# A split-precision cross-attention kernel: seventeen products per context piece in place of eighteen, a stacked last tile, and a new order at the seam

## The reference

```python
def mha(q, k, v):            # 8 heads, softmax(q k^T / sqrt(80)) v
    ...
enc, ca = ctx[:, :718], ctx[:, 718:]
hs = mha(x @ Wq, enc @ Wk, enc @ Wv)
ca_q1 = einsum('btc,th->bch', ca, Wq_ca)[:, linspace(0, 383, 100)]
ca_hs1 = mha(ca_q1, x, x)
ca_hs2 = mha(ca_hs1 @ Wq, ca @ Wk_ca, ca @ Wv_ca)
out = (hs + ca_hs2) @ Wout + b_out + x
```

## Time and profile before

| | us |
|---|---|
| median of 3 runs | 1008.68 |
| lowest and highest | 1005.97, 1013.66 |
| profiled execution, its own time | 1004.1 |
| its span, first to last instruction | 1002.4 |
| TensorE busy | 983.8 (98%) |
| VectorE, ScalarE, GpSimd busy | 645.5, 490.0, 343.5 |
| mean granted TensorE clock | 0.992 |

### The profile page before, as it was taken

The page is one execution under the profiler, slowest core; times in us unless marked ns, Lnnn a source line. Parts: engine busy times, 40 slices in busy tenths (PEclk is TensorE's granted clock), DMA queues, the critical chain, the costliest instruction groups (busy, mean ns, idle before and its releaser), DMA issues.

```text
span 1002.4 us, 20729 instructions
## 1 busy us (share of the span) xinstructions
PE 983.8 (98%) x6740; PEld 964.2 (96%) x6740; DVE 645.5 (64%) x1129; ACT 490.0 (49%) x895; POOL 343.5 (34%) x286
## 2 busy tenths in 40 slices
PE   9999799999999999999999999999999999999998
PEld 9998699999999999999999999999999999998997
DVE  6444556676667766767676767676766666667444
ACT  7433445555454546464646463646454545546110
POOL 5212254424251616151524243343343343416000
PEclk9899999999999999999999999999999999999999
DMA  7989967797978797979797978888787878795354
GB/s 266 258 285 279 259 131 203 168 196 172 195 172 191 174 182 178 185 184 179 185 186 176 186 191 169 202 174 201 161 208 157 206 163 202 168 216 156 97 181 146
DMA packets 154169, 190.12 MB, mean 190 GB/s; under 512 B 80928, under 2 KB 108192, under 8 KB 154144
## 3 DMA queue, kind: packets, MB, share of 16 engines
q1 hardware_dynamic: 147456, 177.44, 75.9%
q10 hardware_dynamic: 6688, 12.35, 3.7%
HBM read 81.56 MB, written 19.95 MB: 101 GB/s over the span
## 4 chain that ended last, share of the span: by engine, by line
PE 85%; SPq 5%; DMA 4%; DVE 3%; ACT 2%; issue 1%; ACTq 0%
PE psS L750 22%; PE psB L785 20%; PE psB L790 10%; PE psS L725 8%; PE psT L766 6%; PE psS L894 6%; PE psT L812 4%; PE psT L818 2%; SPq L382 2%; DMA kstack<-kT 1%; PE psB L867 1%; PE psB L844 1%; SPq L379 1%; PE psT L819 1%; PE psS L950 1%
## 5 line engine op out<-in xcount | busy, mean ns | idle before, releaser
L750 PE MATMUL psS<-encT_keep,Wk_keep 128*128 128x360 f32 x1440 | 255.3, 330 | 2.8 <-ACT probs L1133 2.8
L750 PEld LDWEIGHTS psS<-encT_keep,Wk_keep 128*128 128x128 f32 x1440 | 238.7, 189 | 3.9 <-issue 3.3
L785 PE MATMUL psB<-PT_h,encN_h 120*128 120x400 f32 x576 | 202.3, 351 | 0.0
L785 PE MATMUL psB<-PT_l,encN_h 120*128 120x400 f32 x576 | 198.8, 345 | 0.0
L1133 ACT ACTIVATE probs<-psS,negmax 100x718 f32<-100x718 f32 x128 | 110.2, 861 | 131.8 <-DVE negmax L1524 131.6
L612 POOL TENSOR_TENSOR encT_keep<-encT_raw,encT_keep 128x718 fp32r<-128x718 f32 x45 | 79.7, 1770 | 184.6 <-ACT encT_keep L1162 182.2
L1548 DVE TENSOR_TENSOR kT<-psS,kT 128x718 fp32r<-128x718 f32 x80 | 72.4, 905 | 105.7 <-ACT kT L1157 105.7
L620 POOL TENSOR_TENSOR encN_l<-enc_raw,encN_h 120x768 fp32r<-120x768 f32 x48 | 92.4, 1926 | 93.5 <-ACT encN_h L1169 92.1
L603 POOL TENSOR_TENSOR Mbd<-Mbd,fmask 128x320 fp32r<-128x320 f32 x48 | 47.0, 978 | 221.4 <-DMA Mbd<-m_split 218.8
L1157 ACT ACTIVATE kT<-psS 128x718 fp32r<-128x718 f32 x80 | 61.7, 771 | 123.4 <-PE psS L750 109.9
L790 PE MATMUL psB<-PT_h,encN_l 120*128 120x400 f32 x576 | 120.4, 344 | 0.7 <-POOL encN_l L620 0.7
(11 more groups left out here) (245 smaller groups left out, 1635.8 us busy)
## 6 DMA issues: line engine op xcount, KB each, us to landing
kstack<-kT SPq DMA_DIRECT2D x64, 448.8 KB
kstack<-kT SPq DMA_DIRECT2D x192, 112.2 KB
enc_raw<-in_encN_dram SPq DMA_DIRECT2D x48, 360.0 KB, 5.5
encT_raw<-in_encT_dram SPq DMA_DIRECT2D x45, 359.0 KB, 6.0
kstack<-kT SPq DMA_DIRECT2D x32, 359.0 KB
kstack<-kT SPq DMA_DIRECT2D x32, 269.2 KB
kstack<-kT SPq DMA_DIRECT2D x32, 179.5 KB, 3.6
kstack<-kT SPq DMA_DIRECT2D x64, 89.8 KB, 3.9
```

Source lines behind the costliest of these rows:

```text
L750: mm = pe.matmul(keys_in(f, first)[:, half, 0:HALF], w[:, c, f * 128:(f + 1) * 128], e[:, c, k0:k0 + HALF], start=(j == 0), stop=(j == 3 * ...
L785: pe.matmul(psB[:, 1, 0:RH], eN[0][:, k, cc], PT[p][:, k, rows], start=(k == 0 and p == 0), stop=False)
```

## The change

Key tiles become 128 keys: five full ones (FULLK = 5) and a tail of TAIL = 78. The tail's three products (high-high, high-low, low-high) are folded into two by stacking: rows 78 to 116 of the tail tile, which were unused, hold half of the third product. So `context` has 5 x 2 + 5 + 2 = 17 products. For that

- `norm` writes the first 39 tail keys a second time beside the tail (a new small VectorE instruction for each head), so that the transposes bring them to rows 78 to 116;
- `enc_high` takes key tiles 4 and 5 first (`third`), `enc_twice` (ScalarE) writes the tail's high part into the low buffer too, `enc_low` (GpSimd) has four instructions and makes the tail's low part in place first;
- two DMAs on SP (`tail_enc`) put the tail's low part into the unused rows of both context buffers, one on SP (`tail_pt0`) and one on ScalarE's queue (`tail_pt1`) put 39 rows of the high probabilities into `PT[1]`, for either half of the heads; `context` waits for them just ahead of its last two products (u = 0 for the context, u = 0 and 3 for the probabilities).

Besides: SP issues `load_q(i + 1)` ahead of `lift(i + 1, 0)`; `scores(i, 1)` with its maximum and exponential moves behind `context(i - 1, 2)`; in batch 0 the loads of the next contexts take their ordinary places between the lifts, and `expo(0, 5)` goes ahead of `q_high(3, 5)`; the forty small products are dealt out 7, 7, 7, 7, 6, 6; the context of batch 0 is loaded into another buffer, as soon as Wk has left it, and split ahead of heads 6 and 7.

```diff
-KP = (KEYS + KT - 1) // KT
+KP = 128
-HALF = KPAD // 2
+HALF = 360
+FULLK = KEYS // KP
+TAIL = KEYS - FULLK * KP
+TH = TAIL // 2
+TSTK = TAIL + TH
...
+        LOWS = PARTS + 1
+        tail_low = enc_raw[0:KP, FULLK * C:KT * C].bitcast(F32R)
-        enc0_raw = P_keep[:, 0:CT * KEYS].rearrange("p (c k) -> p c k", c=CT)
+        enc0_raw = rawT
...
+        def third(c):
+            return slice(4, 6) if c == 0 else slice(2 * (c - 1), 2 * c)
...
                 def load_enc(b, c, first=False):
-                    free("encN", PARTS * (b - 1) + c + 1, first)
-                    ks = slice(c * KQ, (c + 1) * KQ)
+                    free("encN", LOWS * (b - 1) + c + 2, first)
+                    if c == 0:
+                        free("entail", 32 * b, first)
+                    ks = third(c)
...
+                def tail_pt0(b):
+                    wait_apart(sp, s["ptlo"], HEADS * b + 4, s["passed_sp"])
+                    sp.dma_start(raw(PT[1][TAIL:TSTK, FULLK, 0:RH]), raw(PT[0][TH:TAIL, FULLK, 0:RH]))\
+                      .then_inc(s["pttail"], 16)
+                def tail_enc(b):
+                    wait_apart(sp, s["encN"], LOWS * b + 1, s["passed_sp"])
+                    for p in range(2):
+                        sp.dma_start(raw(eN[p][TAIL:TSTK, FULLK, :]), raw(tail_low[p * TH:(p + 1) * TH, :]))\
+                          .then_inc(s["entail"], 16)
...
                 load_ga(0, first=True)
+                sp.wait_ge(s["wlo"], 5)
+                sp.dma_start(enc0_raw, encT[0].rearrange("(c p) k -> p c k", p=128)).then_inc(s["encin"], 16)
                 sp.wait_ge(s["hlo"], 6)
                 load_heads(6, 2)
                 sp.wait_ge(s["v2st"], 32)
                 load_q(0, first=True)
-                sp.wait_ge(s["hlo"], HEADS)
-                sp.dma_start(enc0_raw, encT[0].rearrange("(c p) k -> p c k", p=128)).then_inc(s["encin"], 16)
...
                 lift(0, 2, heads=(3,), first=True)
-                sp.wait_ge(s["wlo"], 5)
-                for c in range(CT):
-                    load_encT(1, c, first=True)
-                for c in range(PARTS):
-                    wait_apart(sp, s["xTlo2"], 3 * FT, s["passed_sp"])
-                    load_enc(0, c, first=True)
-                load_ga(1)
+                sp.wait_ge(s["enc0lo"], CT)
...
                     if first:
                         sp.wait_ge(s["encT"], PARTS)
                         sp.dma_start(wv_raw, tiled(Wv)).then_inc(s["wvin"], 16)
                         load_q(i + 1)
-                    else:
+                    tail_pt0(i)
+                    tail_enc(i)
+                    if not first:
                         wait_apart(sp, s["hsp"], 2 * i, s["passed_sp"])
                         load_v2(i)
                         if not last:
                             store_hs(i - 1, 1)
                     if not last:
-                        lift(i + 1, 0)
                         if not first:
                             load_q(i + 1)
+                        lift(i + 1, 0)
                         lift(i + 1, 1)
...
                 def enc_low(b):
-                    for c in range(PARTS):
...
+                    pool.wait_ge(s["encNhi"], LOWS * b + 2)
+                    nc.gpsimd.tensor_tensor(tail_low, rawN[:, FULLK, :], eN[0][:, FULLK, :],
+                                            ALU.subtract).then_inc(s["encN"], 1)
+                    pool.wait_ge(s["encN"], LOWS * b + 1)
+                    nc.gpsimd.tensor_tensor(eN[1][:, FULLK - 1, :], rawN[:, FULLK - 1, :], eN[0][:, FULLK - 1, :],
+                                            ALU.subtract).then_inc(s["encN"], 1)
+                    for c in range(1, PARTS):
...
-                for c in range(3):
+                for c in range(2):
                     wo_low(c)
                 enc_low(B - 1)
...
-                    for k in range(KT):
+                    for k in range(FULLK):
                         for p in range(2):
                             pe.matmul(psB[:, 1, 0:RH], eN[0][:, k, cc], PT[p][:, k, rows],
                                       start=(k == 0 and p == 0), stop=False)
-                    for k in range(KT):
-                        if u == 0 and k % KQ == 0:
-                            pe.wait_ge(s["encN"], PARTS * i + k // KQ + 1)
-                        mm = pe.matmul(psB[:, 1, 0:RH], eN[1][:, k, cc], PT[0][:, k, rows],
-                                       start=False, stop=(k == KT - 1))
-                    mm.then_inc(s["u"], 1)
+                    for n, k in enumerate((4, 0, 1, 2, 3)):
+                        if u == 0 and n in (0, 1, 3):
+                            pe.wait_ge(s["encN"], LOWS * i + (n + 1) // 2 + 2)
+                        pe.matmul(psB[:, 1, 0:RH], eN[1][:, k, cc], PT[0][:, k, rows], start=False, stop=False)
+                    if u == 0:
+                        pe.wait_ge(s["entail"], 32 * i + 32)
+                    if c == 0:
+                        pe.wait_ge(s["pttail"], 32 * i + 16 * half + 16)
+                    pe.matmul(psB[:, 1, 0:RH], eN[0][0:TSTK, FULLK, cc], PT[0][0:TSTK, FULLK, rows],
+                              start=False, stop=False)
+                    pe.matmul(psB[:, 1, 0:RH], eN[1][0:TSTK, FULLK, cc], PT[1][0:TSTK, FULLK, rows],
+                              start=False, stop=True).then_inc(s["u"], 1)
...
                         context(i - 1, 2)
+                        scores(i, 1)
                     keys(i, 3)
...
                         b2_scores(i + 1, 1)
-                        scores(i + 1, 1)
...
+                def enc_twice(b):
+                    nc.scalar.activation(eN[1][0:TAIL, FULLK, :], rawN[0:TAIL, FULLK, :], ACT.Copy)\
+                      .then_inc(s["encNhi"], 1)
+                def tail_pt1(b):
+                    act.wait_ge(s["ptlo"], HEADS * b + HEADS)
+                    act.dma_start(raw(PT[1][TAIL:TSTK, FULLK, RH:R]), raw(PT[0][TH:TAIL, FULLK, RH:R]))\
+                      .then_inc(s["pttail"], 16)
...
                     if first:
                         store_q2(4, FT)
                         store_g2()
+                    else:
+                        u_high(i - 1, 2)
+                        expo(i, 1)
+                    k_high(i, 3)
...
                     xm_copy(i)
+                    expo(i, 5)
                     if first:
                         q_high(3, 5)
                         enc_high(i, 0, first)
+                        enc_twice(i)
                         store_q3(5)
-                    expo(i, 5)
...
+                    nc.vector.tensor_scalar(P[h % PRING][0:S, KEYS:KEYS + TH],
+                                            P[h % PRING][0:S, FULLK * KP:FULLK * KP + TH], inv[:, h:h + 1],
+                                            None, ALU.mult).then_inc(s["inv"], 1)
...
                         u_low(i - 1, 2)
+                        rowmax(i, 1)
+                    k_low(i, 3)
                     norm(i, 1)
-                    k_low(i, 3)
```

More of the change, by code:

```diff
@@ L497, in batch @@
                         load_enc(i, 1)
-                    elif not first:
-                        load_encT(i + 1, 1)
+                    else:
+                        load_encT(i + 1, 1, first)
                     if not first:
@@ L513, in batch @@
                         load_wo(1)
-                    elif not first:
-                        load_enc(i, 1)
-                        load_enc(i, 2)
-                    if not last and not first:
+                    else:
+                        load_enc(i, 1, first)
+                        load_enc(i, 2, first)
                         load_ga(i + 1)
-                    if not last:
                         load_x(i + 1)
@@ L1081, in _ @@
                 turn_ca_keys()
-                for j, heads in enumerate(((0,), (1, 2), (3,), (4,), (5,), (6, 7))):
+                parts = (0, 7, 14, 21, 28, 34, 40)
+                for j in range(NP):
                     query(1, j)
-                    for h in heads:
-                        m_head(h)
+                    m_parts(parts[j], parts[j + 1])
                 query(2, 0)
@@ L1296, in batch @@
                 def batch(i, first=False, last=False):
-                    if not first:
-                        u_high(i - 1, 2)
-                    k_high(i, 3)
                     if first:
@@ L1449, in _ @@
                 q_high(1, 2)
+                for c in range(CT):
+                    enc0_high(c)
                 head_high(6)
@@ L1453, in _ @@
                 q_high(1, 4)
-                for c in range(CT):
-                    enc0_high(c)
                 q_high(1, FT)
@@ L1807, in _ @@
                 q_low(1, 2)
+                for c in range(CT):
+                    enc0_low(c)
                 head_low(6)
@@ L1811, in _ @@
                 q_low(1, 4)
-                for c in range(CT):
-                    enc0_low(c)
                 q_low(1, FT)
```

65 lines of the change are left out of this document (38 added, 27 removed).

## The result

| | before | after |
|---|---|---|
| median (4 runs each) | 1009.95 | 1051.91 |
| lowest and highest | 1005.97, 1013.66 | 1038.95, 1059.53 |
| ratio, 95% interval | | 1.038 [1.0335, 1.0425] |
| span of the profiled execution | 1002.4 | 1037.2 |
| mean granted TensorE clock | 0.992 | 0.976 |

A forecast was written before the change was run, and what follows sets the result against it. TensorE was taken as the bound inside the loop. Fewer products (-17.6), the net of (a) to (e) (-5.8) and the last batch (+0.5) gave -22.9 from 1004.1, 981.2; plus 4.6 for the median, 985 us, range 974 to 1000.

The forecast's parts named there:

- The tail's DMAs in the loop: SP's three tail loads per batch, wanted by the stacked products: slack 1.4 to 3 us, later SP issues covered by 5; nothing.
- q ahead of lift 0: SP's loop order: last lift piece just in time for keys 2; nothing, bounds 0.1 us gain to 1 us loss per batch.
- Rival 1: Every batch: late lifts or a late exponential cost 0.5 to 1 us in 15 batches, total 993 to 1000; chance 0.13.
- third rival: Context 0, products 16 and 17: tail DMAs late in every batch, slow clock after, 57 us in all, total 1042; chance 0.07.
- Scores 1 behind a context piece: Loop, scores 1 moved: exponential 1 still ready for scores 2 with 0.4 to 1 us to spare; zero gain or loss.
- One product less: Each context piece on TensorE: one product fewer, 16 batches x 6 pieces x 0.184 = 17.6 us saved, bounds 17 to 18.
- (c): Before keys 3 of batch 0: exponential 5 moved ahead removes the 2.81 wait and slow products after it, -4.6 us.
- (e): Batch 0, context 0: new wait of 4.2 us for the tail's DMAs behind q, plus slow stretch, +5.8 us (2.5 to 7).
- (d): Forty small products before batch 0, dealt in even lots: part of the clock loss from 34 to 46 us regained, -1.5 (0 to -3.4).
- (a): Batch 0's context loaded and split elsewhere: ends the wait at 81.79 and the slow stretch after it, -3.8 us (0 to -4.2).
- (b): Batch 0, lift 2 (head 4): bulk loads no longer ahead of it, -1.7 us of the wait at 105.47 (0 to -3).
- Last batch: Context 0 of the last batch wants GpSimd's split parts 0.5 us earlier: costs 0.5 us (0 to 2).

## Why the prediction was wrong, step by step

**The tail's DMAs in the loop: the step that failed.** The landing was right (the wait stands in batch 0 alone). The sentence behind it was wrong: "Queued behind this wait on SP are V2, the output store, q and lift 0, whose first issue starts only at 549.93: covered by 5 us." It set 544.8 against 549.93 and left out V2 and the store between them, 2.5 and 0.4 us and their gaps. The cover was the 1.5 us in which SP stood still, against three issues of 0.8 with gaps, 2.6 us in all, where 0.48 each had been read from a load of another shape. Lift 0 began 1.1 to 1.3 us later against TensorE. That the queue ahead of the lift is the cause is shown by the kernel that keeps q ahead and only moves V2 and the store (with GpSimd's spread of V2): -41.5 us. In the kernel with the products alone the same lateness makes q late in place of the lift, and the loop gains nothing (730.0 for 729.1).

**q ahead of lift 0.** "Just in time" was nearly right for SP as it stood before: the copy of keys 2 was 1.0 us later, and the total some 5 us longer. But the margin was 0.1 us and the step before had already spent it. The two hang together: with q put back, or V2 and the store out of the way, 40 us come back (1051.9 to 1011.5 or 1010.4). I summed two terms of zero, each worked out with the other's slack unspent.

**Rival 1** named this chain and priced it at 0.5 to 1 us per batch; it was 53.86 - 50.85 = 3.0 against the forecast period; 0.7 of this is the 51.57 that its best batch reached, where the moved scores 1 have their part. The price lacked the stretch at the low clock: 2.2 us of waiting had 2.7 of slow products behind it. The third rival had that factor, for another wait; that its 1042 came near the measured time is luck, for the stacked products of the loop never waited.

**Scores 1 behind a context piece.** Zero was wrong: 0.5 to 0.6 us per batch alone (52.57 for 52.08 in the mean, and 52.55 for 51.92 in the steady batches). The text asked only what scores 1 would wait for, not what had been running beside it in its old place. With turn 7 in the gap the wait goes.

**One product less, transposes, small VectorE instruction.** Right: 0.17 to 0.18 per piece and 51.0 as the lowest period, against 50.85. By the Trainium skill ("TensorE: Matmul & The Clock Gate", LDWEIGHTS), which has the load's time as columns / 1.2 ns, each load would be an estimated 7 ns longer. The traces show nothing of it in the pace: six transposes still take 0.46 from their start to that of the next instruction. The 39-column instruction takes 0.25 alone but 1.08 beside GpSimd, so "surely under 0.56" was wrong there.

**The seam.** (c) right, no wait at keys 3 of batch 0. (e) right in place and near in the wait, 4.86 for 4.2, but the slow stretch behind it was 7.9 us at a granted clock of 0.51, an estimated 3.9 lost in place of 1.6; repaired by order. (d) the granted clock from 34 to 46 us rose from 0.72 to 0.96, but from 46 to 58 it fell from 1.00 to 0.89. (a) right at its place: where 2.07 of waiting and slow products stood at 81.79, scores 0 of batch 0 now follow at once and at full pace:

```profile
79.66 0.34 PE L868 MATMUL psB<-gbd,a 128*100 128x400 f32 x1
79.84 0.33 PE L755 MATMUL psS<-kstack,qstack_h 120*100 120x360 f32 x1
```

What (a) left out lies ahead of that: the first stretch was 77.9 to 79.8 in the four profiled kernels with the old order and 77.1 to 85.4 in thirteen with the new one. (b) was not tried by itself; ScalarE's wait of 1.95 for the lift is gone, but TensorE has one of 1.66 at 107.81 in its stead. Batch 0 took 58.1 to 61.8 with (e) repaired, 2.5 to 6 less than before, where the terms (a) to (c), which fall into it, had 10.1. Where the rest stayed is open.

**Last batch.** 0.5 (0 to 2) was forecast, 8.4 measured in the changed kernel and 5.8 with q behind. There ScalarE stood 4.0 us at the high part of Wout (1.4 before), whose load is issued behind the longer queue, and two divisions ran beside GpSimd, as two had before. Repaired, 0.8 to 1.8 us stay. But a kernel without any repair there (V2 and the store late, q ahead) had 2.7 only, so how the 5.8 divide is open.

## What to carry over

Slack in an in-order queue is the time in which it stands still, counted from the last instruction ahead of the one that matters. When several edits draw on one slack, add them before you compare. Before an instruction is moved, ask also what it covers: the drain of a bank, or the wait of another queue. A wait of 1 to 2 us of TensorE in a tight loop should be priced with the slow stretch behind it.

## What was not expected of the hardware

- A VectorE instruction of 39 columns, 0.25 us alone, takes as long as 1.08 beside GpSimd: in a busy stretch the size of an instruction says little of its time.
- Two waits of 1.38 and 0.81 us, 1.7 us apart from start to start, were followed by a context piece of 5.8 us at the lower clock. Behind the single wait of 4.86 in batch 0 the slow products lasted from 133.01 to 140.90, 7.9 us.
- The first stretch differs by up to 8 us between profiled executions of kernels with the same code there (77.1 to 85.4), so one profile does not price it. The granted clock from 58 to 70 us was 1.00 in the shortest and 0.53 in the longest.
